# Increments of TensorE's results carried by drain instructions, in two adjacency layers

## The reference

```
h = relu(layernorm(x))
Qn, Kn = cos_normalize(h @ Wq.T), cos_normalize(h @ Wk.T)
att = softmax(where(adj > 0, Kn @ Qn.T, NEG), axis=1)
prop = att @ h                                # h itself for a row without neighbours
x = x + 0.5 * prop + 0.5 * h
h = relu(layernorm(x))
g = h @ W.T + b_W
e = leaky_relu((g @ a1)[:, None] + (g @ a2)[None, :] + b_a, 0.2)
x = x + softmax(where(adj > 0, e, NEG), axis=1) @ g
```

## Time and profile before

| what | value |
|---|---|
| median of three timed runs | 1603.69 us |
| span of the profiled execution, first to last instruction | 1797.8 us |
| TensorE busy (matmuls) | 1091.8 us, 61% |
| TensorE busy (weight loads, beside them) | 826.5 us, 46% |
| VectorE, ScalarE busy | 1053.4 us, 965.5 us |
| GpSimd busy | 1092.0 us, 61% |
| mean granted clock of TensorE | 0.797 |
| moved by DMA | 358.43 MB |

### The profile page before, as it was taken

The page is one execution under the profiler, slowest core; times in us unless marked ns, Lnnn a source line. Parts: engine busy times, 40 slices in busy tenths (PEclk is TensorE's granted clock), DMA queues, the critical chain, the costliest instruction groups (busy, mean ns, idle before and its releaser), DMA issues.

```text
span 1797.8 us, 21638 instructions
## 1 busy us (share of the span) xinstructions
PE 1091.8 (61%) x5729; PEld 826.5 (46%) x5729; DVE 1053.4 (59%) x4249; ACT 965.5 (54%) x2795; POOL 1092.0 (61%) x1121
## 2 busy tenths in 40 slices
PE   6883878687867776787756305444444544454546
PEld 4651545455544554555446105444333444344445
DVE  6974678768776777687765114434444444444446
ACT  4653657677766667676667504443433443343334
POOL 1355666666666656566663675766666666666671
PEclk9996879889888887888887556867778767777778
DMA  9998989799979997999921221222222222222221
GB/s 368 421 377 313 345 323 399 289 342 389 393 262 347 358 364 253 344 367 369 360 51 37 52 54 41 55 51 51 52 51 52 54 52 52 51 51 52 53 52 28
DMA packets 90472, 358.43 MB, mean 199 GB/s; under 512 B 23653, under 2 KB 36328, under 8 KB 57576
## 3 DMA queue, kind: packets, MB, share of 16 engines
q1 hardware_dynamic: 49128, 277.05, 39.2%
q0 software_dynamic: 34304, 71.42, 15.2%
q10 hardware_dynamic: 6912, 8.52, 1.3%
HBM read 344.18 MB, written 12.72 MB: 199 GB/s over the span
## 4 chain that ended last, share of the span: by engine, by line
issue 32%; PE 26%; POOL 17%; DVE 7%; ACT 6%; another core or an unknown queue 6%; DMA 5%; SPq 0%; ACTq 0%; POOLq 0%; DVEq 0%
PE ps L580 14%; POOL arena L965 9%; POOL arena L973 6%; DMA arena<-in_adj_dram 3%; PE ps L557 2%; PE ps L1027 2%; PE ps L567 2%; ACT prod L1215 2%; DMA arena<-tab,idx_shared 2%; PE ps L1050 2%; PE ps L1008 1%; ACT diag L1234 1%; POOL arena L542 1%; DVE arena L1443 1%
## 5 line engine op out<-in xcount | busy, mean ns | idle before, releaser
L965 POOL DMA_INDIRECT arena<-tab,idx_own x320 | 329.8, 1030 | 164.5 <-issue 86.5
L580 PE MATMUL ps<-arena,diag 128*128 128x130 f32 x640 | 143.5, 402 | 406.9 <-issue 405.2
L542 POOL DMA_INDIRECT arena<-tab,idx_own x320 | 308.6, 964 | 97.5 <-issue 97.5
L580 PEld LDWEIGHTS ps<-arena,diag 128*128 128x128 f32 x640 | 127.9, 299 | 448.8 <-issue 446.2
L1027 PE MATMUL ps<-arena,fold 128*128 128x512 fp8e4 x1024 | 299.4, 438 | 33.4 <-DMA arena<-in_adj_dram 22.3
L537 POOL DMA_INDIRECT arena<-tab,idx_shared x216 | 206.0, 954 | 181.5 <-remote 101.8
L973 POOL DMA_INDIRECT arena<-tab,idx_shared x216 | 208.9, 967 | 154.3 <-DVE idx_shared L1493 84.3
L600 ACT COPY arena<-ps 128x512 f32<-128x512 f32 (+1 forms) x120 | 52.9, 489 | 459.2 <-remote 395.2
L1050 PE MATMUL ps<-arena,R 128*128 128x154 f32 x736 | 144.8, 357 | 108.5 <-ACT R L1187 38.4
L1215 ACT ACTIVATE prod<-prod,arena 128x128 f32<-128x128 f32 x528 | 203.4, 390 | 0.0
L1050 PEld LDWEIGHTS ps<-arena,R 128*128 128x128 f32 x736 | 133.0, 239 | 133.0 <-issue 50.8
(11 more groups left out here) (200 smaller groups left out, 2348.3 us busy)
## 6 DMA issues: line engine op xcount, KB each, us to landing
arena<-in_adj_dram SPq DMA_DIRECT2D x256, 1024.0 KB
arena<-tab,idx_own POOLq DMA_INDIRECT x640
arena<-tab,idx_shared POOLq DMA_INDIRECT x432
tab<-arena ACTq DMA_DIRECT2D x16, 260.0 KB, 7.3
tab<-tw ACTq DMA_DIRECT2D x32, 130.0 KB
res<-in_x_dram SPq DMA_DIRECT2D x8, 512.0 KB, 11.7
out_dram<-arena SPq DMA_DIRECT2D x64, 64.0 KB
prod<-in_L_gnn_Wq_dram SPq DMA_DIRECT2D x1, 64.0 KB
```

Of the source, the lines that this page charges most:

```text
L542: pool.indirect_dma_start(out=GO[q][:, s, :], out_offset=None, in_=tab1, in_offset=bass.IndirectOffsetOnAxis(ap=idx_own[:, t, s:s + 1], ax ...
L580: last = nc.tensor.matmul(out_ps[p][:, 0:ROW], lhs, rhs, start=s == 0, stop=s == K + n - 1)
L965: pool.indirect_dma_start(out=G[t % GR][:, s, :], out_offset=None, in_=tab0, in_offset=bass.IndirectOffsetOnAxis(ap=idx_own[:, t, s:s + 1] ...
```

## The change

At seven places TensorE's increment moves from the last matmul of a group to a drain instruction put behind it. A drain is an instruction of the engine's sequencer that ends when what was issued before it on that engine is done.

```diff
             def edge_scores(t):
...
-                last = nc.tensor.matmul(T_ps[t % 4][:, 0:n * P], column[:, 0:1].to_broadcast([P, P]),
-                                        on_diag[t % 2][:, 0:n, :], start=True, stop=True)
-                last.then_inc(s_T, 1)
+                nc.tensor.matmul(T_ps[t % 4][:, 0:n * P], column[:, 0:1].to_broadcast([P, P]),
+                                 on_diag[t % 2][:, 0:n, :], start=True, stop=True)
+                pe.drain().then_inc(s_T, 1)
             def transposes(t):
...
-                last.then_inc(s_tr1, 1)
+                pe.drain().then_inc(s_tr1, 1)
             def weighted(t):
...
-                last.then_inc(s_pv1, 1)
+                pe.drain().then_inc(s_pv1, 1)
...
                 def folds(t, first=0, end=PIECES):
...
                         for b in range(PIECE_BITS):
-                            last = nc.tensor.matmul(keys_ps[t % 2], fold[:, PIECE_BITS * f + b, :],
-                                                    ring8[m % RING][:, b * WORDS:(b + 1) * WORDS],
-                                                    start=False, stop=PIECE_BITS * f + b == BITS - 1)
-                        last.then_inc(s_piece, 1)
+                            nc.tensor.matmul(keys_ps[t % 2], fold[:, PIECE_BITS * f + b, :],
+                                             ring8[m % RING][:, b * WORDS:(b + 1) * WORDS],
+                                             start=False, stop=PIECE_BITS * f + b == BITS - 1)
+                        pe.drain().then_inc(s_piece, 1)
...
                 def owners(t):
...
-                        last.then_inc(s_E, 1)
+                        pe.drain().then_inc(s_E, 1)
                 def weighted(t):
...
-                    last.then_inc(s_pv, 1)
+                    pe.drain().then_inc(s_pv, 1)
                 def weighted_last(t):
...
-                    last.then_inc(s_pv, 1)
+                    pe.drain().then_inc(s_pv, 1)
```

More of the change, by code:

```diff
@@ L566, in transposes @@
                 for c in range(n):
-                    last = nc.tensor.transpose(WT_ps[c // 4][:, c % 4 * P:(c % 4 + 1) * P],
-                                               sc[p][:, K + c * P:K + (c + 1) * P], ident[:, :])
-                last.then_inc(s_tr1, 1)
+                    nc.tensor.transpose(WT_ps[c // 4][:, c % 4 * P:(c % 4 + 1) * P],
+                                        sc[p][:, K + c * P:K + (c + 1) * P], ident[:, :])
+                pe.drain().then_inc(s_tr1, 1)
             def weighted(t):
@@ L579, in weighted @@
                     rhs = GO[q][:, s, :] if s < K else GS[:, (C * h + first + s - K) % CR1, :]
-                    last = nc.tensor.matmul(out_ps[p][:, 0:ROW], lhs, rhs, start=s == 0, stop=s == K + n - 1)
-                last.then_inc(s_pv1, 1)
+                    nc.tensor.matmul(out_ps[p][:, 0:ROW], lhs, rhs, start=s == 0, stop=s == K + n - 1)
+                pe.drain().then_inc(s_pv1, 1)
             edge_scores(0)
@@ L1049, in owners @@
                                 at = c - SPAN[w % QT][0]
-                                last = nc.tensor.matmul(E_ps[g % 2][:, k * REC:(k + 1) * REC], R[w % 2][:, at * P:(at + 1) * P],
+                                nc.tensor.matmul(E_ps[g % 2][:, k * REC:(k + 1) * REC], R[w % 2][:, at * P:(at + 1) * P],
                                                         owner[:, w, :], start=w == of[0], stop=w == of[-1])
-                        last.then_inc(s_E, 1)
+                        pe.drain().then_inc(s_E, 1)
                 def weighted(t):
```

## The result

In runs beside each other the kernel before took 1601.89 us (median of 5) and the changed one 1608.40 us (median of 5). The ratio is 1.0037, 95% interval 1.0026 to 1.0047: 6.5 us slower, between 4.2 and 7.5. The forecast was 10.3 us slower, 1614 against 1603.7.

What follows compares the result with a forecast made beforehand. Transfers were taken to bound the adjacency stage (710 us) and GpSimd's gathers the second layer (676 us). Timed: 1603.7 + 10 for first-layer drains - 0 for late increments = 1614 us; own range 1599 to 1640, with rivals 1515 to 1660.

Steps and rivals of the forecast that it cites:

- Late increments go with GpSimd's gathers: Beside the gathers, a matmul's increment can reach its waiter 4.5 us after the matmul's end; before and after them it is prompt.
- The sum that excluded late increments from timed runs: Whole kernel: stage times 120 + 710 + 95 + 772 + 31 = 1728 us, or 1632 with GpSimd's floor, both above 1603.69.
- The span forecast for the change, 1671 us: Traced execution of the changed kernel: 1797.8 - 102 (second layer) - 35 (adjacency stage) + 10 (drains) = 1671 us.
- What a drain costs TensorE: Each drain among matmuls: 0.387 + 0.04 + 0.10 restart - 0.223 = 0.30 us of lost overlap, between 0 and 0.55.
- my estimate of 0.16 us: Cost of a drain on TensorE by the skill page's figures for a matmul alone and in a stream, 398 columns more.
- I let one eighth through: 10 us: Adjacency stage: 354 drains, 106 us of TensorE, 79 delaying real work, of which 10 us lengthen the kernel; ends 0 and 79.
- I cost them at 0, at most 16 us: The first layer's remaining 54 drains, at the adjacency stage's edges, where TensorE waits for loads or the last gathers: 0.
- the ring of six pieces: Adjacency stage: a late piece delays the load six pieces ahead, some 3 us each, so DMAs cover about 18 us.
- Costed at 0 because GpSimd hides it: Second layer: 192 drains, 58 us, raise TensorE's cycle from 6.0 to 6.9 us a tile, below GpSimd's 10.6: 0.
- A: Rival, chance 0.33: increments are late in timed runs too and drains cure it; 1603.7 - 83 + 10 = 1531 us.
- B: Rival, chance 0.15: TensorE bounds the adjacency stage, once remaining waits there exceed 0.5 us a tile; 1643 us.
- C: Rival, chance 0.10: drains wait for late increments of some 96 matmuls that keep theirs; 43 us more, 1657 us.

## Why the prediction was right or wrong, point by point

**What bounds the kernel.** The floors were right in kind. The adjacency stage is bound by its transfers, forecast as 710 us of work and measured at 692 us with a share of 0.99; the second layer by GpSimd's gathers, forecast as 676 us and measured at 691 to 694. "Late increments go with GpSimd's gathers" held in that execution alone. Increments of the seven places stood on matmuls beside gathers in nine more traced executions, and in none was one late.

**How that execution stands to the timed ones.** The sum that excluded late increments from timed runs (1728 us with them, 1632 without, against 1603.69) was the step that carried the forecast, and its conclusion was right, though its terms came from the odd execution (the second trace has 692, 80, 691 and 15 us where it put 710, 95, 676 and 31). What I drew from it, that increments are late "mostly when the execution is traced", was wrong: tracing alone is not the cause, since the same kernel traced again has a span of 1598.2 us. That a span 194 us above the median marks a disturbed execution was in reach. The signs that I set for "right", no remote waits and a second layer of about 680 us, came true, but they show nothing of the drains: the second trace of the kernel before has them too. The span forecast for the change, 1671 us, was too long by 64 for the same reason: I took off what I could name and left the rest of that execution in.

**What a drain costs TensorE.** Forecast 0.30 us, at least 0 and at most 0.55. Eight fold matmuls with one drain among them take 2.22 us in the changed kernel; at 0.223 us from start to start they would take 7 x 0.223 + 0.387 = 1.95 us without it.

```profile
503.58 2.22 PE L1027 MATMUL ps<-arena,fold 128*128 128x512 fp8e4 x8
```

That is 0.27 us by these rounded rows. Over the trace a fold matmul behind a drain starts 0.467 us after the one ahead of it, and 0.226 without one: 0.24 us. The 0.04 us to the drain's end and the 0.10 us of the restart were 0.02 and 0.06. The Trainium skill's overlap rule (TensorE: Matmul & The Clock Gate, section "Step-by-step: what each phase is for") was right in direction; my estimate of 0.16 us from that page's figures lies below the measured 0.24, and the fixed 0.30 above.

**First layer: the step that failed in size.** "I let one eighth through: 10 us" of 79. What came through in this stage is 2.6 us by the traces, and the pieces' drains cost 4.2 us (2.2 to 6.1) by time. The rest of the 6.5 us comes from terms that I costed at 0: 1.5 us from the drains at the edge of the stage ("I cost them at 0, at most 16 us") and some 2.2 us from the second layer. One term too large and two too small brought the total as near as it is, and that is luck. The 354 drains of the stage are 354 x 0.24 = 85 us, and TensorE's waits there fell by about as much: for loads from 98.8 to 35.8 us, for masks (L1050 for L1187) from 37.1 to 19.0, for offsets (L1035) from 21.9 to 11.9, 91 us in all. I had looked for the cover in the ring of six pieces and called it 18 us. The cover is TensorE's own wait for loads, and in the trace that I read that wait was small:

```profile
PE ps L1027 <- DMA arena<-in_adj_dram: 14.6, 4, 10.2
PE ps L1027 <- issue: 9.6, 11, 2.5
```

There TensorE stood ahead of L1035 and L1050 instead, for 164.4 of its 201 idle us with "issue" counted in, of which the earlier trace rows are the two longest. The eighth was a choice and not worked out; with the wait of the second trace, nearly nothing should come through at 256 drains, and the run with 256 more shows that the last part of a slack is not used up cleanly: 12 us come through while 11.7 us of waits are left.

**Second layer.** Costed at 0 because GpSimd hides it: ratio 1.0005, 0.9997 to 1.0014. Right for the 58 us that it hid; the 1.0 us after the last gather, where no gather is left to hide a drain, was in no term. Where GpSimd was made to wait for TensorE, the forecast's 0.9 us a tile was about 0.45, the drain ahead of the sum; that the other two drains cost that cycle next to nothing is read from the two timelines and not from a run of its own.

**The rivals.** A, faster, fell: no increment is late in timed runs, and the drains' own kernel is the slower one when increments are on the path. B, TensorE as the bound, is what the runs with more drains show; at the change's own number it had not come to that. Its form was right and its 0.5 us was that of the odd execution. By the second trace a tile (692 us for 890 folds, 55.6 tiles) needs 0.99 x 692 / 55.6 = 12.3 us of the DMAs and, with the change's drains, (539.2 + 85) / 55.6 = 11.2 of TensorE, and the waits for masks and offsets that remain are 30.9 / 55.6 = 0.6 us, less than the 1.1 to spare. With 256 more drains TensorE needs 12.2 us, and the stage begins to grow; with 768 more it needs 14.1, and it is the bound. C had nothing to act on, as no increment was late; it stays untested.

**The chances.** 0.45 for slower by over 0.3% went to what happened, at 0.37%, with the interval's low end at 0.26%, so it stands at the edge between slower and the same. The 0.32 for faster rested on lateness that only the odd execution had.

## What to carry to other kernels

Compare the profiled execution's span with the timed runs before reading its waits: a span 11% above the median called for a second trace, and every remote wait of the first one was gone in it. A drain among matmuls costs TensorE what one matmul's tail and the next weight load overlap, here 0.24 us for folds and 0.45 us ahead of a float32 sum; it is hidden as long as TensorE waits for something anyway, and paid in full once that wait is used up. To find out how far a cost is from being paid, add more of it: two kernels with more drains told more than six that took drains away.

## What the runs showed of the hardware that was not expected

In one traced execution, increments of matmuls reached their waiters up to several us late (4.5 us in the earlier trace rows) while GpSimd gathered, and the same program traced again, and eight others with such increments, showed none. ScalarE's increments were prompt in it: in the earlier trace rows the sum starts 0.10 us after the copy that releases it (1308.11 to 1308.21). The recording of that execution also holds only 10225 updates of semaphores, where that of the second holds 29920 for the same 21638 instructions, some two thirds fewer. Whether the recording disturbed the execution or suffered with it is not shown, and the cause is open.

The granted clock of TensorE in the adjacency stage did not fall with the drains. It was 0.92 in the second trace of the kernel before, 0.94 with the change, and 0.95 and 0.94 with more drains. In these traces losses of 0.24 us a drain stand where waits of up to 3.0 us for loads stood; whether that is the reason is not shown.
